# Rows folded by symmetry behind the row transforms, column transforms as fp32 pairs in array halves

## The chip, the core and the metric
The kernel runs on one core of one Trainium2 chip. TensorE (PE in the profile) multiplies matrices, its weight loads are listed as PEld; VectorE is DVE, ScalarE is ACT, GpSimd is POOL, and SyncE (SP) issues DMAs, the copies between DRAM and on-chip memory (SBUF; TensorE writes into PSUM). All times are device microseconds (us). The metric is the time of one execution of the whole program. fp32r is a single-pass form of fp32 on TensorE with less precision; fp32 proper takes two instructions of two passes each per product.

## The reference
Input x is (8, 56, 56, 256), fp32: eight images of 56 rows of 56 positions, 256 channels. One block of three residual layers is computed; the change is in the first.

```python
x = x + conv(_gn(x), ...)            # group normalisation, then the layer below
t = tokens(x)
t = t + attention(_ln_t(t), ...)     # not touched
t = t + ffn(_ln_t(t), ...)           # not touched

def conv(x, ...):
    xn = simple_rms(x)
    u = silu(xn @ W_u.T + b_u)       # 512 channels, a gate
    v = silu(xn @ W_v.T + b_v)       # 512 channels
    g = rpe_coeffs(...)              # small MLP over the 111 x 111 offsets: 512 numbers each
    a = zeros(112, 112); a[offsets mod 112] = g
    vf = rfft2(v, s=(112, 112)); af = rfft2(a)
    y = irfft2(vf * af)[:56, :56]    # per channel: a long convolution over the image
    return (u * y) @ W_o.T + b_o + x
```

The Fourier transforms are matrix products with cosines and sines. Only 56 of the 112 row frequencies are carried, each as a real and an imaginary plane, so a transformed image has 112 rows (ROWS) for 56 (SIDE).

## The kernel before
The program is six phases, one after another, with a barrier of all engines between them; each phase writes its results to DRAM for the next. Within a phase every engine has its own instruction list, written out by hand in the order in which it runs, and semaphores tie the lists together. The change touches the first four phases.

**Kernel rows** (`kernel_rows_phase`, names kr_). The MLP runs over all offsets in 14 steps of eight rows, `u` = 0 and 1 of four (RPE_ROWS) each. GpSimd casts the coordinates of four rows (`take_points`, L306), TensorE's `first_layer` (L383) takes them, deeper layers follow, with scales that VectorE computes in a chain of small operations (L547 to L559). The tail of a step has eight rows: TensorE makes the coefficients, VectorE adds the bias (L649) and makes the low part (L633, both inputs in SBUF), TensorE transforms along the row (`row_pass`), ScalarE copies out (`take_row`, L487), and SP stores four rows at a time (L296, kern_rows). Group normalisation's statistics are taken beside it.

**Project** (`project_phase`, pr_). 56 chunks of eight image rows, four tiles `t` of two rows each. GpSimd normalises (L1047, L1051), TensorE transposes (L1064) and multiplies with W_v, VectorE scales and adds the bias (L1220, here "bias"), ScalarE applies silu (L1142, "gate"), TensorE transforms along the row: one product for each of the tile's two rows, on array row halves (L1084, contraction over 56 partitions, from 0 and from 64). ScalarE copies out one row (L1148), VectorE the other (L1228), and SP stores the chunk (L1004, v_rows). VectorE also makes low parts of the transposed x (L1212, twice a chunk).

**Columns** (`columns_phase`, co_). For each of 56 row frequencies k: the taps of the convolution's kernel are transformed along the column (four products of 111 x 512 into `taps_ps`), ScalarE copies them to `spec`. For each image b of eight: forward column transform, product with the spectrum (complex: VectorE multiplies L902 and L904, GpSimd subtracts and adds L925 and L928), inverse transform (L806, L808), copy (ScalarE L862), store. The forward and taps products go as high and low fp32r parts, three passes each by the helper `product` (L135): ScalarE makes the high part (L837, L841), VectorE the low (L882, L887). SP loads v (L736) and taps (L732), and stores y (L742) for each pair of images.

**Mix** (`mix_phase`, mx_). 56 chunks again: x is loaded and normalised anew on GpSimd (L1429, L1433), the gate u is made, TensorE transforms back along the row (L1485, array column halves), VectorE multiplies with the gate (L1710), TensorE transposes (L1495) and multiplies with W_o, and residual and layer norm follow (residual: GpSimd L1442, L1445).

## Time and profile before

| | |
|---|---|
| median of 3 runs | 5410.76 us (5406.27 to 5413.85) |
| profiled execution | span of its instructions 5398.1 us, its only time |
| kernel rows | first 690 us |
| project | to about 1285 us |
| columns | to about 2860 us |
| mix | to about 3930 us |
| busy over the span | PE 97%, DVE 74%, ACT 47%, POOL 46% |

The profile is of one execution. In a line of the page's groups, `L902 DVE TENSOR_TENSOR co_direct<-co_v_ps,co_spec ... x448` is line 902 of the program, the engine, the operation, what it writes and reads, and how often it ran; then the busy time, the mean of one in ns, and the time the engine was idle before it. In a timeline the first number is the start, the second how long the group of instructions ran; an engine can overlap the end of one operation with the start of the next, so that starts of VectorE's operations stand closer than their durations. An idle time with an arrow names who ended it.

### The profile page before, as it was taken

Reading aid. Unit: us, or ns where it says so; the run is one execution under the profiler, and the core shown is the slowest. Engines: PE = TensorE matmul, PEld = TensorE weight load, DVE = VectorE, ACT = ScalarE, POOL = GpSimd, SP = SyncE. Lnnn points to the kernel's source line nnn. Section 1 sums busy time; section 2 is a strip of 40 time slices with the busy share of each in tenths; the row PEclk is TensorE's granted clock in tenths of the full one; section 3 lists DMA queues with packets and bytes.
Section 4 is the critical chain, followed back from the end, with each engine's and each line's share of the span. In section 5 each row is a group of like instructions: output and inputs, shape, how many; then the busy total and the mean of one; then the engine's idle time right before and its main releaser. Section 6 shows DMA issues by size and latency. Waiting matters only on the chain. (4 is left out here: it accounts for less than half of the span.)

```text
span 5398.1 us, 89326 instructions
## 1 busy us (share of the span) xinstructions
PE 5214.1 (97%) x27048; PEld 3662.3 (68%) x27048; DVE 3997.7 (74%) x6176; ACT 2512.3 (47%) x4791; POOL 2489.9 (46%) x1381
## 2 busy tenths in 40 slices
PE   8999899997999999999998999999989999987999
PEld 6777655554555555555556777777767777765999
DVE  6777666666999999999996676766635666665887
ACT  5555577774434334343434555555532222211555
POOL 0000054443999999999995555555301111111332
PEclk9999999998999999999999999999999999998999
DMA  3222167775444444444446666666533333433443
GB/s 109 89 89 72 53 197 219 217 217 170 149 150 150 149 152 148 152 148 150 151 136 182 195 203 200 191 200 202 163 113 97 104 113 107 118 89 97 123 122 113
DMA packets 349121, 782.62 MB, mean 145 GB/s; under 512 B 43433, under 2 KB 147845, under 8 KB 339460
## 3 DMA queue, kind: packets, MB, share of 16 engines
q1 hardware_dynamic: 326596, 703.91, 44.2%
q10 hardware_dynamic: 22400, 77.08, 4.0%
q8 instruction: 73, 1.20, 0.1%
q14 instruction: 52, 0.43, 0.0%
HBM read 420.49 MB, written 360.38 MB: 145 GB/s over the span
## 5 line engine op out<-in xcount | busy, mean ns | idle before, releaser
L928 POOL TENSOR_TENSOR co_prod<-co_cross 111x512 f32<-111x512 f32 x448 | 848.8, 1895 | 0.0
L862 ACT ACTIVATE co_y_out<-co_y_ps 112x512 f32<-112x512 f32 x448 | 267.9, 598 | 928.2 <-PE co_y_ps L808 923.1
L925 POOL TENSOR_TENSOR co_prod<-co_direct 111x512 f32<-111x512 f32 x448 | 576.3, 1286 | 203.8 <-PE co_y_ps L808 116.0
L902 DVE TENSOR_TENSOR co_direct<-co_v_ps,co_spec 111x1024 f32<-111x1024 f32 x448 | 543.5, 1213 | 92.0 <-PE co_v_ps L135 87.9
L2012 POOL TENSOR_TENSOR at_t<-at_t,at_p_bias 112x1024 f32<-112x1024 f32 x56 | 137.7, 2470 | 889.3 <-DMA at_t<-t_tiles 889.3
L904 DVE TENSOR_TENSOR co_cross<-co_v_ps,co_spec 111x1024 f32<-111x1024 f32 x448 | 541.5, 1209 | 0.0
L135 PE MATMUL co_v_ps<-co_v_high,co_col_fwd_high 112*111 112x512 f32 x896 | 506.1, 565 | 1.4 <-DVE co_cross L904 1.4
L806 PE MATMUL co_y_ps<-co_prod,co_col_inv 111*112 111x512 f32 x896 | 458.2, 592 | 0.0
L808 PE MATMUL co_y_ps<-co_prod,co_col_inv 111*112 111x512 f32 x896 | 457.5, 592 | 0.1
L882 DVE TENSOR_TENSOR co_v_low<-co_v_in,co_v_high 112x1024 fp32r<-112x1024 f32 x224 | 372.3, 1662 | 0.0
L135 PE MATMUL co_v_ps<-co_v_low,co_col_fwd_high 112*111 112x512 f32 x896 | 354.3, 395 | 0.0
L2173 ACT ACTIVATE at_qk_t<-at_bank_ps 128x448 f32<-128x448 f32 x224 | 121.6, 543 | 499.1 <-PE at_bank_ps L135 499.1
L135 PE MATMUL co_v_ps<-co_v_high,co_col_fwd_low 112*111 112x512 f32 x896 | 349.1, 390 | 0.0
L1596 ACT ACTIVATE mx_mixed_high<-mx_turn_ps 128x448 fp32r<-128x448 f32 x224 | 121.8, 544 | 431.1 <-PE mx_turn_ps L1495 431.1
L808 PEld LDWEIGHTS co_y_ps<-co_prod,co_col_inv 111*112 111x112 f32 x896 | 156.0, 175 | 229.3 <-issue 212.3
L1220 DVE SCALAR_TENSOR_TENSOR pr_v_pre<-pr_v_ps,pr_inv,pr_v_bias 120x512 f32<-120x512 f32 x224 | 167.6, 748 | 150.8 <-PE pr_v_ps L135 145.5
L1442 POOL TENSOR_TENSOR mx_resid<-mx_x_in,mx_o_bias 112x1024 f32<-112x1024 f32 x56 | 134.0, 2393 | 311.2 <-DVE mx_t L1726 311.2
L306 POOL CAST kr_points<-kr_coords 6x448 fp32r<-6x448 f32 x28 | 15.2, 568 | 565.8 <-DMA kr_coords<-coords 565.8
L2502 POOL TENSOR_TENSOR ff_base<-ff_t,ff_n 112x1024 f32<-112x1024 f32 x56 | 132.7, 2370 | 301.3 <-DVE ff_out L2663 281.5
L1047 POOL TENSOR_TENSOR pr_gx<-pr_x_in,gn_rows 128x1024 f32<-128x1024 f32 x55 | 133.0, 2419 | 298.1 <-DMA pr_x_in<-x 298.1
L135 PE MATMUL mx_o_ps<-mx_w_o_high,mx_mixed_high 128*112 128x256 f32 x896 | 252.3, 282 | 3.5 <-DVE mx_mixed_low L1715 3.5
L135 PE MATMUL mx_o_ps<-mx_w_o_high,mx_mixed_low 128*112 128x256 f32 x896 | 252.2, 281 | 0.0
(277 smaller groups left out, 14268.5 us busy)
## 6 DMA issues: line engine op xcount, KB each, us to landing
v_rows<-pr_rows_out SPq DMA_DIRECT2D x56, 1792.0 KB, 8.2
co_v_in<-v_rows SPq DMA_DIRECT2D x448, 224.0 KB
y_rows<-co_y_out SPq DMA_DIRECT2D x448, 224.0 KB
mx_y_in<-y_rows SPq DMA_DIRECT2D x224, 448.0 KB, 5.5
kr_x_in<-x SPq DMA_DIRECT2D x56, 448.0 KB, 3.9
kern_rows<-kr_rows_out SPq DMA_DIRECT2D x28, 896.0 KB, 4.7
pr_x_in<-x SPq DMA_DIRECT2D x112, 224.0 KB
mx_x_in<-x SPq DMA_DIRECT2D x56, 448.0 KB, 5.3
```

What stands on the lines that cost most here:

```text
L135: last = nc.tensor.matmul(out, weights[a], data[b], start=start and i == 0, stop=stop and i == len(passes) - 1)
L806: nc.tensor.matmul(y_ps[b % 2][:2 * SIDE, :], col_inv[:, 0, :], prod[b % 2][:, :WIDE], start=True, stop=False)
L808: nc.tensor.matmul(y_ps[b % 2][:2 * SIDE, :], col_inv[:, 1, :], prod[b % 2][:, WIDE:], start=False, stop=True).then_inc(inv_mm, 1)
L862: nc.scalar.activation(y_out[:, b, :], y_ps[b % 2][:2 * SIDE, :], ACT.Copy).then_inc(y_ready, 1)
L882: nc.vector.tensor_tensor(v[1][:, images, :], v_in[:, images, :], v[0][:, images, :].bitcast(F32), ALU.subtract).then_inc(low_v, 1)
L902: nc.vector.tensor_tensor(direct[b % 2][:], v_ps[b % 2][:POINTS, :], spec[i][:, :2 * WIDE], ALU.mult).then_inc(real_terms, 1)
L904: nc.vector.tensor_tensor(cross[b % 2][:], v_ps[b % 2][:POINTS, :], spec[i][:, WIDE:], ALU.mult).then_inc(multiplied, 1)
L925: nc.gpsimd.tensor_tensor(prod[b % 2][:, :WIDE], direct[b % 2][:, :WIDE], direct[b % 2][:, WIDE:], ALU.subtract).then_inc(real_ready, 1)
L928: nc.gpsimd.tensor_tensor(prod[b % 2][:, WIDE:], cross[b % 2][:, :WIDE], cross[b % 2][:, WIDE:], ALU.add).then_inc(combined, 1)
L1220: nc.vector.scalar_tensor_tensor(out=v_pre[t % 2][:], in0=v_ps[t % 2][:SPAN, :], scalar=inv[:SPAN, j % GROUP * TILES + t:j % GROUP * TILES ...
L1442: nc.gpsimd.tensor_tensor(resid[u][:], x_in[u][:], o_bias[:].unsqueeze(1).to_broadcast(each), ALU.add).then_inc(resid_part, 1)
L2012: nc.gpsimd.tensor_tensor(t1[j % HELD][:], t1[j % HELD][:], p_bias[:].unsqueeze(1).to_broadcast([TILE, TILES, CH]), ALU.add).then_inc(t1_b ...
```

## The change
The image rows are reordered on the host, so that each chunk of eight rows holds mirrored pairs (row i and row 55 - i), and back on the way out. A row transform's result of a pair is then folded: the sum goes to one slot, the difference to another. The fold of the sum has a real plane, that of the difference is written with real and imaginary planes exchanged, so that a store of a chunk is three DMAs. The offsets of the kernel are ordered in mirrored pairs as well.

With folded rows the forward column transform needs one product over 56 rows for each of the two halves of the input, not a complex one over 112, and likewise the inverse.

- Kernel rows: GpSimd folds (`fold_rows`, two operations of 112 x 1024 for four rows) from `rows_out` into `taps_out`; SP stores `taps_out` in three pieces; ScalarE's `take_row` waits for the fold.
- Project: the row product writes 1024 columns per tile; ScalarE copies an even tile (`take_first`), VectorE adds and subtracts the odd one (`fold_rows`, two operations of 112 x 1024). The normalised x (gx) is stored too.
- Columns: no high and low parts. The forward transform is two fp32 products over 56 partitions each (0 to 55 and 64 to 119, array row halves), the inverse two products of 56 output columns (array column halves), the taps two full fp32 products. VectorE multiplies once per image, 2048 columns, with the PSUM operand repeated; GpSimd adds once, 1024 columns. For image 5 GpSimd does nothing and TensorE sums the terms in PSUM with four products. Rings of four, lag of three images. ScalarE copies four parts of the spectrum.
- Mix: gx is loaded, not computed. The odd result is copied by ScalarE (`take_odd`), VectorE adds and subtracts (`unfold`, 4 operations of 120 x 512 a chunk), GpSimd multiplies with the gate (`mix`, four of 120 x 512). TensorE has the same products in another order.

```diff
# kernel rows, GpSimd
+                def fold_rows(s, u):
+                    n = s * 2 + u
+                    pool.wait_ge(row_out, RPE_ROWS * (n + 1))
+                    pool.wait_ge(stored[u], 16 * PIECES * s)
+                    pair = rows_out[u][:].rearrange("p (m r) n -> p m r n", r=2)
+                    for parity, op in enumerate((ALU.add, ALU.subtract)):
+                        nc.gpsimd.tensor_tensor(taps_out[u][:, parity * MIRRORS:(parity + 1) * MIRRORS, :], pair[:, :, 0, :],
+                                                pair[:, :, 1, :], op).then_inc(folded, 1)
+
                 for s in range(STEPS):
                     for u in range(2):
                         take_points(s, u)
+                        if s:
+                            fold_rows(s - 1, u)
+                for u in range(2):
+                    fold_rows(STEPS - 1, u)
# project, VectorE and ScalarE
-                def take_row(s, j, t):
-                    nc.vector.tensor_copy(rows_out[j % 2][:, 2 * t + 1, :], row_ps[t % 2][1][:ROWS, :]).then_inc(row1_out, 1)
+                def fold_rows(s, j, pair):
+                    dve.wait_ge(first_out, 1 + n + 1)
+                    dve.wait_ge(row_mm, 2 * n + 2)
+                    nc.vector.tensor_tensor(out[:, slots(0, pair), :].rearrange("p r n -> p (r n)"), first[pair][:],
+                                            row_ps[1][:ROWS, :], ALU.add)
+                    nc.vector.tensor_tensor(out[:, slots(1, pair), :].rearrange("p r n -> p (r n)"), first[pair][:],
+                                            row_ps[1][:ROWS, :], ALU.subtract).then_inc(folded, 1)
+                def take_first(s, j, pair):
+                    act.wait_ge(row_mm, 2 * n + 1)
+                    act.wait_ge(folded, n)
+                    nc.scalar.activation(first[pair][:], row_ps[0][:ROWS, :], ACT.Copy).then_inc(first_out, 1)
# columns, SP
+                def stored(k, pair):
+                    sp.wait_ge(y_ready, SLOTS + k * BATCH + 2 * pair + 2)
+                    store_y(sp, k, pair)
                 def step(k, i, more, more2):
                     for pair in range(PAIRS):
+                        if more and pair + 1 < PAIRS:
+                            next_v(k, 1, pair + 1)
+                        if more2 and pair + 1 == PAIRS:
+                            sp.wait_ge(taps_mm, k + 2)
                             load_taps(sp, k, 2)
+                            next_v(k, 2, 0)
+                        stored(k, pair)
# columns, TensorE
+                    for part in range(2):
+                        side = slice(part * GAP, part * GAP + SIDE)
+                        last = nc.tensor.matmul(v_ps[b % 2][:POINTS, bass.ts(part, WIDE)], col_fwd[side, :], v_in[side, b, :],
+                                                start=True, stop=True)
+                        for part in range(2):
+                            last = nc.tensor.matmul(y_ps[b % 2][part * GAP:part * GAP + SIDE, :],
+                                                    col_inv[:, part * SIDE:(part + 1) * SIDE],
+                                                    prod[b % RING][:, bass.ts(part, WIDE)], start=True, stop=True)
                     for b in range(LAG, BATCH):
-                        if b == BATCH // 2 + 1 and more:
-                            spectrum(k + 1)
+                        if more and b <= LAG + 1:
+                            spectrum(k + 1, b - LAG)
                         forward(k, b)
                         inverse(k, b - LAG)
# columns, VectorE and GpSimd
+                        twice = [POINTS, 2, 2 * WIDE]
+                        nc.vector.tensor_tensor(terms[b % RING][:].rearrange("p (t n) -> p t n", t=2),
+                                                v_ps[b % 2][:POINTS, :].unsqueeze(1).to_broadcast(twice),
+                                                spec[i][:].rearrange("p (t n) -> p t n", t=2), ALU.mult).then_inc(multiplied, 1)
+                    for b in POOLED:
+                        pair = terms[b % RING][:].rearrange("p (t s n) -> p t s n", t=2, s=2)
+                        nc.gpsimd.tensor_tensor(prod[b % RING][:].rearrange("p (t n) -> p t n", t=2), pair[:, :, 0, :], pair[:, :, 1, :],
+                                                ALU.add).then_inc(combined, 1)
```

GpSimd's list in kernel rows, before: nothing but casts of coordinates, one for each `u`.

```order
L306 CAST kr_points0<-kr_coords0 6x448
L306 CAST kr_points1<-kr_coords1 6x448
L306 CAST kr_points0<-kr_coords0 6x448
L306 CAST kr_points1<-kr_coords1 6x448
L306 CAST kr_points0<-kr_coords0 6x448
```

And of the changed kernel, from its first step on:

```order
L336 CAST kr_points0<-kr_coords0 6x448
L336 CAST kr_points1<-kr_coords1 6x448
L336 CAST kr_points0<-kr_coords0 6x448
L344 ISA
L344 TENSOR_TENSOR kr_taps_out0<-kr_rows_out0 112x1024 x2
L336 CAST kr_points1<-kr_coords1 6x448
L344 TENSOR_TENSOR kr_taps_out1<-kr_rows_out1 112x1024 x2
L336 CAST kr_points0<-kr_coords0 6x448
```

From the second step on, a fold of the step before stands between the cast of points 0 and that of points 1.

VectorE's list in project, before (L1220 is the bias, L1212 the low parts, L1228 the copy of row results; register instructions are waits whose value is computed):

```order
L1220 SCALAR_TENSOR_TENSOR pr_v_pre<-pr_v_ps,pr_inv,pr_v_bias 120x512
L1209 REGISTER_ALU
L1212 TENSOR_TENSOR pr_x_t_low<-pr_xt_ps,pr_x_t_high 128x480 x2
L1218 REGISTER_ALU
L1220 SCALAR_TENSOR_TENSOR pr_v_pre<-pr_v_ps,pr_inv,pr_v_bias 120x512
L1227 REGISTER_ALU
L1228 COPY pr_rows_out<-pr_row_ps 112x512 x2
L1218 ISA
L1220 SCALAR_TENSOR_TENSOR pr_v_pre<-pr_v_ps,pr_inv,pr_v_bias 120x512
L1218 REGISTER_ALU
L1220 SCALAR_TENSOR_TENSOR pr_v_pre<-pr_v_ps,pr_inv,pr_v_bias 120x512
L1228 COPY pr_rows_out<-pr_row_ps 112x512 x2
```

And of the changed kernel (L1259 is the bias, L1251 the low parts, L1270 and L1272 the fold):

```order
L1259 SCALAR_TENSOR_TENSOR pr_v_pre<-pr_v_ps,pr_inv,pr_v_bias 120x512
L1257 REGISTER_ALU
L1259 SCALAR_TENSOR_TENSOR pr_v_pre<-pr_v_ps,pr_inv,pr_v_bias 120x512
L1265 REGISTER_ALU
L1266 ISA
L1270 TENSOR_TENSOR pr_rows_out<-pr_first,pr_row_ps 112x1024
L1272 TENSOR_TENSOR pr_rows_out<-pr_first,pr_row_ps 112x1024
L1257 REGISTER_ALU
L1259 SCALAR_TENSOR_TENSOR pr_v_pre<-pr_v_ps,pr_inv,pr_v_bias 120x512
L1248 REGISTER_ALU
L1251 TENSOR_TENSOR pr_x_t_low<-pr_xt_ps,pr_x_t_high 128x480 x2
L1257 REGISTER_ALU
```

The fold stands where the two copies stood, twice as wide, and reads what ScalarE's `take_first` wrote.

SP's list in columns, before, around a taps load (L732; L736 loads v, L742 stores y):

```order
L732 DMA co_taps_in<-kern_rows 111x512
L732 ISA
L732 DMA co_taps_in<-kern_rows 111x512
L716 REGISTER_ALU
L742 ISA
L742 DMA y_rows<-co_y_out 56x2x512
```

And of the changed kernel (L770 taps, L774 v, L780 y):

```order
L780 DMA y_rows<-co_y_out 56x2x512
L780 ISA
L780 DMA y_rows<-co_y_out 56x2x512
L805 REGISTER_ALU
L770 ISA
L770 DMA co_taps_in<-kern_rows 112x512
L770 ISA
L770 DMA co_taps_in<-kern_rows 112x512
L793 ISA
L774 ISA
L774 DMA co_v_in<-v_rows 56x2x512
```

Before, the load is ahead of the store of images 2 and 3 and asks for low parts made early in the frequency; now it stands behind the store of images 4 and 5 and ahead of the next frequency's first v load.

## Rows read from the trace of the kernel before

**Rows 1.** Windows: length; busy PE, PEld, DVE, ACT, POOL; PE clock, DMA share, GB/s
```profile
0.00:690.00 690.00, 649.26 (x4618) 492.03 (x4620) 486.90 (x997) 368.94 (x713) 31.81 (x42) 0.99 0.28 83
690.00:1285.00 595.00, 580.86 (x2648) 343.82 (x2648) 382.41 (x609) 458.23 (x1060) 251.77 (x105) 0.99 0.69 213
1285.00:2860.00 1575.00, 1546.67 (x5156) 900.14 (x5156) 1459.04 (x1185) 617.19 (x900) 1405.17 (x901) 0.99 0.48 148
2860.00:3930.00 1070.00, 1043.65 (x6716) 797.95 (x6716) 726.70 (x1515) 593.19 (x1008) 530.74 (x223) 0.99 0.66 194
```

**Rows 2.** The taps tile: instructions, ns min/median/max, first and last start
```profile
L732 SPq MOVE co_taps_in<-kern_rows x108: 29/29/29, 1319.3 to 2779.2; - x108
```

**Rows 3.** Timeline of columns, 2000 to 2030: start, length, instructions
```profile
2002.40 1.02 PE L806 MATMUL co_y_ps<-co_prod,co_col_inv 111*112 111x512 f32 x2
...
2004.32 0.60 ACT L862 ACTIVATE co_y_out<-co_y_ps 112x512 f32<-112x512 f32 x1 [2.50 <-PE co_y_ps L808]
...
2005.09 0.88 SPq L742 DMA_DIRECT2D y_rows<-co_y_out  x2
...
2005.49 1.02 PE L806 MATMUL co_y_ps<-co_prod,co_col_inv 111*112 111x512 f32 x2
```

**Rows 4.** The v_rows tensor: its stores in project, first and last start
```profile
L1004 SPq DMA_DIRECT2D v_rows<-pr_rows_out x56: 316/356/364, 697.8 to 1271.8; - x56
```

**Rows 5.** Timelines of project, from 1001, and of mix, from 3504
```profile
1004.42 1.21 DVE L1212 TENSOR_TENSOR pr_x_t_low<-pr_xt_ps,pr_x_t_high 128x480 fp32r<-128x480 f32 x2
...
1005.03 1.97 PE L1084 MATMUL pr_row_ps<-pr_v,pr_row_fwd 56*112 56x512 f32 x8
...
1006.94 0.50 PE L135 MATMUL pr_v_ps<-pr_w_v_high,pr_x_t_high 128*120 128x512 f32 x1
...
3506.71 1.93 PE L1485 MATMUL mx_y_ps<-mx_y_in,mx_row_inv 112*56 112x512 f32 x8
```

**Rows 6.** Groups by line and shape: count, busy us, mean ns, idle before
```profile
L902 DVE TENSOR_TENSOR co_direct<-co_v_ps,co_spec 111x1024 f32<-111x1024 f32 x448 | 543.5, 1213 | 92.0 <-PE co_v_ps L135 87.9 <-ACT co_spec L846 4.1
...
L928 POOL TENSOR_TENSOR co_prod<-co_cross 111x512 f32<-111x512 f32 x448 | 848.8, 1895 | 0.0
...
L1442 POOL TENSOR_TENSOR mx_resid<-mx_x_in,mx_o_bias 112x1024 f32<-112x1024 f32 x56 | 134.0, 2393 | 311.2 <-DVE mx_t L1726 311.2
```

**Rows 7.** Timeline of columns, 2016 to 2021, VectorE and GpSimd
```profile
2016.50 1.30 POOL L925 TENSOR_TENSOR co_prod<-co_direct 111x512 f32<-111x512 f32 x1 [0.57 <-PE co_y_ps L808]
...
2016.94 1.93 DVE L882 TENSOR_TENSOR co_v_low<-co_v_in,co_v_high 112x1024 fp32r<-112x1024 f32 x1
...
2017.76 2.27 POOL L928 TENSOR_TENSOR co_prod<-co_cross 111x512 f32<-111x512 f32 x1
```

**Rows 8.** The page's DMA issues: count, KB each, median us from issue to landing
```profile
n_tok<-mx_n ACTq DMA_DIRECT2D x56, 448.0 KB, 3.1
...
mx_y_in<-y_rows SPq DMA_DIRECT2D x224, 448.0 KB, 5.5
```

**Rows 9.** Groups by line and shape: bias, gate and a wide ScalarE read of PSUM
```profile
L1220 DVE SCALAR_TENSOR_TENSOR pr_v_pre<-pr_v_ps,pr_inv,pr_v_bias 120x512 f32<-120x512 f32 x224 | 167.6, 748 | 150.8 <-PE pr_v_ps L135 145.5 <-DVE pr_inv L1205 5.2
...
L1142 ACT ACTIVATE pr_v<-pr_v_pre 120x512 f32<-120x512 f32 x222 | 140.0, 631 | 120.8 <-DVE pr_v_pre L1220 120.1
...
L470 ACT ACTIVATE kr_square<-kr_t_ps 128x896 f32<-128x896 f32 x112 | 102.8, 918 | 146.7 <-PE kr_t_ps L398 130.0 <-PE kr_t_ps L383 16.6
```

**Rows 10.** Timeline of kernel rows, 288 to 303: end of a step, start of the next
```profile
290.95 0.34 SPq L296 DMA_DIRECT2D kern_rows<-kr_rows_out  x1
...
291.23 0.68 DVE L633 TENSOR_TENSOR kr_coef_low<-kr_coef,kr_coef_high 111x512 fp32r<-111x512 f32 x1
...
294.04 0.49 PE L135 MATMUL kr_row_ps<-kr_coef_high,kr_row_taps_high 111*112 111x512 f32 x1 [0.22 <-DVE kr_coef_low L633]
...
294.93 0.67 PE L383 MATMUL kr_t_ps<-kr_points,kr_w_in_both 6*128 6x448 f32 x2
...
302.15 0.27 DVE L547 SCALAR_TENSOR_TENSOR kr_scale<-kr_scale,kr_root 128x112 f32<-128x112 f32 x1
```

518 lines of the change are left out of this document (254 added, 264 removed).

## The prediction

> **What bounds the kernel now.** I read the stage windows first [rows 1]: in the four stages that the change touches TensorE is busy 649 of 690, 581 of 595, 1547 of 1575 and 1044 of 1070 us, and no other engine comes near it, except in the column stage, where VectorE has 1459 and GpSimd 1405 us. The granted clock is 0.99 in all four, the 2.4 GHz level. So TensorE sets the end everywhere; its work is where time can be won, and the question for the other engines is whether they stay below it. Second, the period of each loop. Columns: a row frequency every 27.55 us (the moves in front of the taps loads, two per frequency, run from 1319.3 to 2779.2 over 54 frequencies: 1459.9/53 [rows 2]); an image every 3.09 us, 2005.49 − 2002.40 [rows 3]. Project: 56 stores from 697.8 to 1271.8, 574.0/55 = 10.44 us a chunk [rows 4]. Kernel rows: 14 steps in the first 690 us, mix: 56 chunks in 1070 us [rows 1].
>
> **Columns: TensorE's work.** An image now costs six single-pass products of 0.23 us and two fp32 products of 0.86 us. After the change both transforms are fp32 pairs in the two halves of the array. How long is such a pair? In the project stage two tiles make eight instructions on row halves from 1005.03 to 1006.94 [rows 5]: 1.91 us for four products of 512 columns; one after another they would take 4 × 0.86 = 3.4, two at a time 1.71, so the halves do run together, and 0.2 is left for the way in and out. Column halves do the same: eight in 1.93 us [rows 5]. I take 0.854 for a pair and 0.17 for each change of array shape. No row shows a change from row halves straight to column halves; the bounds are 0.1 and 0.3.
> Per image: 2 × 0.854 + 2 × 0.17 = 2.05, eight of them 16.4. Image 5 has one more pair, 0.85. The taps' spectrum is two full products, 1.71, and two more changes, 0.34. Sum **19.3 us** a frequency (with 0.1 and 0.3 for a change: 18.0 and 21.6).
>
> **Columns: the others.** VectorE had two products of 1.21 per image [rows 6] and a split of two images' input in every second one. It gets one product of 2048 columns; back-to-back ones of 1024 start 1.13 apart, so 2.20 to 2.28, times eight 17.6 to 18.2: below 19.3, by little. That it reads PSUM twice over is shown by no row; the bounds are 2.2 and, at half speed, 4.4 (rival c), and 2.2 is taken because width alone set the time of the others. GpSimd had 1.30 and 1.90 per image for operations of the same width [rows 6, 7]; the second is long where VectorE's split, with both inputs in SBUF, lies beside it: the split of 2016.94 lasts 1.93 and goes on past the end of GpSimd's at 2017.80, and GpSimd's next, from 2017.76, lasts 2.27 instead of 1.30 [rows 7]. The splits go. One GpSimd operation of 1024 columns takes 2.39 [rows 6]; seven, with 0.1 for each handover, 17.4: below 19.3 too. ScalarE: eight copies of 0.60 and four of the spectrum. Three engines stand within 10% of each other and the ring of four with a lag of three lets them drift, so TensorE stays the bound.
> One wait is new. The taps load of frequency k+2 is issued behind the store of images 4 and 5, and TensorE wants it after image 7's inverse. From the end of inverse 5: ScalarE's copy 0.04 + 0.60, store issue 0.17 later (2004.92 to 2005.09 [rows 3]), 0.88 for its two issues [rows 3], then the load, 448 KB: transfers of that size landed after 3.1 and 5.5 us (medians [rows 8]); I take 3.6, near the lower, as the DMA share here is 0.48 against 0.66 in mix [rows 1]. Together 5.3, with 0.05 more to TensorE 5.4, while TensorE has forward, inverse, forward, inverse, 4 × 1.025 = 4.1. Stall **1.3 us** a frequency (0.8 with 3.1, 3.2 with 5.5). Before, the load had a whole frequency of room.
> So 20.6 a frequency: (27.55 − 20.6) × 56 = −389, and −8 for the splits and the wait for them at the stage's start. Range −479 (19.0 a frequency) to −339 (21.5).
>
> **Project.** TensorE's work stays. The loop that closes is between VectorE and ScalarE. Before, eight copies of 512 columns, four on each, emptied the row product, and each depended only on its own tile. Now ScalarE copies a pair's even tile (1024 columns: 0.918 for 896 [rows 9], so 1.01) and VectorE folds with 2 × 1.13 = 2.26. In the order of the instructions: bias 3 (0.75 [rows 9]) → gate 3 (0.63 [rows 9]) → first 0 (1.01) → fold 0 (2.26) → bias 0 and 1 (1.50) → gate 1 (0.63) → first 1 (1.01) → fold 1 (2.26) → bias 2 (0.75) → low parts (1.21 [rows 5]) → bias 3. Each waits for the one before it, on its engine or by a semaphore: 12.01, and six handovers of 0.04, 12.25 a chunk; with the reciprocal of every second chunk 12.35. Against 10.44 of now that is +1.9, × 56 = **+106**. It would be +40 if part of it hides (the low parts, 1.21, beside a wait of ScalarE), +120 if ScalarE's table loads join it. The stores of three pieces and gx (448 KB a chunk more) go by a queue that waits; the DMA share is 0.69 now [rows 1].
>
> **Kernel rows.** GpSimd gets two operations of 1024 columns per four rows, 4.8 us, twice a step; its own share is small. But its order is cast, fold, cast, fold, so the cast of the next step's second coordinates stands behind the fold. The fold starts when row 4 of the step is out, 290.95, and ends 295.9; with the cast behind it (0.6) TensorE's first layer, which stands at 294.93 [rows 10], starts 1.7 us late. And VectorE's operations with two SBUF inputs did not run beside GpSimd's in the column stage; each waited the other out [rows 7]. At 291.23 the low part of a coefficient, two SBUF inputs, becomes ready beside the fold [rows 10]; it waits to 293.5, GpSimd's second waits 0.7 for it, the next low part waits again to 296.6, and the row product of 294.04 [rows 10] follows at 297.3: 3.3 late, which contains the 1.7. The second fold, from 301.7, meets the scale of a layer (302.15, two SBUF inputs [rows 10]) and costs up to 2.4 more. 5.7 a step × 14 = +80; the last fold and store +5. I take **+82**; bounds +20 (the queue's 1.7 alone, × 14 = 24, some of it hidden) and +100. (The Trainium skill has a rule against this part: SBUF — State Buffer, SBUF: two separate sides, says that the port pair of VectorE and GpSimd is an exclusive lock, held for the whole instruction by whichever of them starts first. The rows at 2016.94 and 2017.76 agree. Where two engines only shared a rate, the wait of the 14 steps would be near the queue's +24 + 5 = +29; by the rule it is the +82 above.)
>
> **Mix.** TensorE's work is the same; GpSimd loses two normalising operations of 2.39 and gets four products of half the width; ScalarE gets 2 × 0.6 beside a half-idle engine (593 of 1070 [rows 1]); the gx load adds 448 KB to a stage at 0.66 of DMA [rows 1]. The gated tile now comes by one more engine (a copy, an unfold, GpSimd's product) but TensorE's order asks for it later. I take +0.2 a chunk, **+12**; bounds −5 and +45.
>
> **Sum.** −389 − 8 + 106 + 82 + 12 = −197. The profiled execution has a span of 5398.1 us; the median of three runs is 5410.76, 12.7 more, for what lies around the span. The change is the same on either: 5398.1 − 197 + 12.7 = **5214 us**.
>
> **Rivals.** (a) *TensorE alone sets it*: no stall for the taps and no lock in kernel rows. Columns 19.3 (−462 − 8), project +60, kernel rows +24 + 5, mix 0: 5030 us. For it: the rings, and that folds are off TensorE. Against it: the order of the queues, and [rows 7]. Chance 0.15.
> (b) *GpSimd sets the columns*: its wide operation takes what its two took together, 1.30 + 1.90 = 3.20 [rows 6, 7]. 7 × 3.2 = 22.4 a frequency, −288 − 8; with the rest, 5315. For it: this is how it runs there now. Against it: VectorE's two-SBUF operations are gone. Chance 0.12.
> (c) *Slower than before*: VectorE's product reads PSUM twice over by a stride of zero. Ran it at half speed, 4.4 an image, a frequency would take 35.2: (35.2 − 27.55) × 56 = +428, and with −8 and the +200 of the other stages 6031 us. The point from which it decides is nearer: the other stages' +200 − 8 = 192 are 3.4 a frequency, so the change loses where a frequency takes more than 24.1, a product of VectorE more than 3.0. Against it: a product's time went by its width in every form seen, 1.21 with PSUM [rows 6]. Chance 0.08.
> (d) *The change doesn't win where it says*: the loops of project and kernel rows take more than the sum (each its upper bound, 120 + 100 + 45 = 265) and the columns 21.5, −339 − 8: 5329. Chance 0.07. My forecast has 0.58.
>
> **Range and chances.** From 5080 (columns at 19.3 with part of the losses outside: −470 + 140 = −330) to 5340 (columns at 21.5 with the losses outside, or rival b and a little). Rival (a)'s core and (c) stay out. Faster by over 0.2% (11 us, about what a measurement tells from no change): all but (c) and 0.01: 0.91; within 0.2%: 0.01; slower 0.08.
>
> **What would show it.** Of the changed kernel: taps loads 20.6 us apart, and TensorE idle about 1.3 before the taps' product with a DMA as releaser; VectorE's product at 2.2 to 2.3, GpSimd's at 2.4; stores of v 12.3 apart; in kernel rows VectorE's low part of a coefficient stretched to 2 us or more, the steps 5.7 longer. Wrong would be: GpSimd's sum over 2.7 (rival b), VectorE's product over 2.5 (rival c), pairs that end 1.7 apart, project at 10.5 (the loop isn't closed), or steps of kernel rows longer by under 2 (the engines' meeting costs nothing).

## The result, and the profile after

The changed kernel takes 5494.41 us (median of four runs, 5492.59 to 5500.43); the kernel before, timed beside it, 5409.88. The ratio is 1.0163, 95% interval 1.0151 to 1.0175: slower by 1.6%. The prediction was 5214, with 5080 to 5340 as its range: wrong in sign and outside the range. The profiled execution has a span of 5494.0 us against 5398.1, so 95.9 us are to be explained. (The prediction added 12.7 us for what lies around the span; here the profiled execution took 5495.8 us, 1.8 more than its span. So about 11 of the 12.7 were the difference between one execution and the median.)

The table sets the stages side by side, each cut at an event that both kernels have (the first move in front of a taps load stands half a frequency later in the changed kernel; cut at the very first taps load, 1280.5 and 1484.3, project would be +117 and columns −218). The middle columns are from the trace, the last is the sum of the prediction.

| stage, cut at | before | after | difference | predicted |
|---|---|---|---|---|
| kernel rows, to the last store of kern_rows | 661.1 | 748.0 | +87 | +82 |
| project, to the first move of the taps loads | 658.2 | 773.2 | +115 | +106 |
| columns, to the first load of y in mix | 1536.8 | 1320.4 | −216 | −397 |
| mix, to the last load of y | 1004.7 | 1106.8 | +102 | +12 |
| what follows (not changed) | 1537.3 | 1545.6 | +8 | 0 |
| sum | 5398.1 | 5494.0 | +96 | −197 |

Two of the four terms came near what was worked out, one of them with some luck, as said below. Two did not, and together they are 271 of the 293 us by which the forecast of the span missed. Windows of the changed kernel by stage (length; busy PE, PEld, DVE, ACT, POOL; clock, DMA share, GB/s), which answer to [rows 1]:

```profile
0.00:760.00 760.00, 669.14 (x4576) 494.26 (x4576) 571.61 (x987) 358.72 (x681) 163.80 (x92) 0.96 0.25 73
760.00:1482.00 722.00, 618.58 (x2688) 347.84 (x2688) 493.57 (x619) 467.22 (x980) 264.30 (x110) 0.98 0.70 214
1482.00:2845.00 1363.00, 1179.46 (x4036) 266.19 (x4036) 1001.84 (x453) 377.45 (x673) 915.90 (x396) 0.92 0.58 172
2845.00:3990.00 1145.00, 1060.01 (x6664) 779.33 (x6664) 719.94 (x1489) 631.70 (x1102) 547.34 (x336) 1.00 0.71 198
```

Before, TensorE was busy in 94 to 98% of each of these stages. Now it is idle for 91, 103, 184 and 85 us of them, no other engine has more than 76% in any, and the granted clock of the columns is 0.92 instead of 0.99. A stage in which no engine is full is set by a chain that passes through several of them.

**Columns.** TensorE's own work is as worked out. The two starts of L855, the inverse transform, are 2.05 us apart, as the sum of four array halves and their changes said; VectorE's product and GpSimd's sum have their expected lengths (groups by line and shape: count, busy us, mean ns, idle before):

```profile
2107.84 1.07 PE L855 MATMUL co_y_ps<-co_prod,co_col_inv 111*56 111x512 f32 x4
...
2109.89 1.07 PE L855 MATMUL co_y_ps<-co_prod,co_col_inv 111*56 111x512 f32 x4
```

```profile
L926 DVE TENSOR_TENSOR co_terms<-co_v_ps,co_spec 111x2048 f32<-111x2048 f32 x448 | 999.8, 2284 | 340.7 <-PE co_v_ps L837 328.0
L944 POOL TENSOR_TENSOR co_prod<-co_terms 111x1024 f32<-111x1024 f32 x392 | 915.3, 2358 | 480.3 <-DVE co_terms L926 478.9
```

With 2284 and 2358 ns both engines wait over 300 us for the one ahead of them: neither rival (b) nor (c) happened. What did is in the tile of the loaded taps (its moves, the register instructions in front of the loads; who waited for it: us, times), and in the timeline around one wait:

```profile
L770 SPq MOVE co_taps_in<-kern_rows x108: 29/29/29, 1521.2 to 2788.4; - x108
...
  PE co_taps_ps L826: 156.5, 55
```

```profile
2101.02 1.97 PE L826 MATMUL co_taps_ps<-co_taps_in,co_col_taps 112*111 112x512 f32 x2 [3.96 <-DMA co_taps_in<-kern_rows]
...
2102.92 1.91 PE L837 MATMUL co_v_ps<-co_v_in,co_col_fwd 56*111 56x512 f32 x4
...
2105.76 1.11 PE L826 MATMUL co_taps_ps<-co_taps_in,co_col_taps 112*111 112x512 f32 x2
...
2106.80 1.11 PE L837 MATMUL co_v_ps<-co_v_in,co_col_fwd 56*111 56x512 f32 x4
```

A frequency takes (2788.4 − 1521.2)/53 = 23.91 us. TensorE waits for the taps 55 times, 2.85 us each. And the first two groups behind the wait take 1.97 and 1.91 where the same instructions take 1.11 later. The windows of this place say why: no matmul from 2098 to 2101, then a granted clock of 0.54, near the lower of its two levels (1.2 GHz), then 1.00 (2.4 GHz) again.

```profile
2098.00:2101.00 3.00, 0.00 (x0) 0.00 (x0) 0.65 (x1) 0.00 (x0) 3.00 (x2) 1.00 0.82 249
2101.00:2104.70 3.70, 3.68 (x6) 0.82 (x6) 0.00 (x0) 0.00 (x0) 0.53 (x1) 0.54 0.21 82
2104.70:2120.00 15.30, 15.30 (x62) 3.53 (x60) 14.21 (x7) 5.53 (x10) 9.83 (x5) 1.00 0.54 156
```

**Mix.** The timeline of one chunk shows which engines hand to each other (start, length, instruction, idle before and releaser). Its first half, around VectorE's shift:

```profile
3492.20 1.28 ACT L1633 ACT_TABLE_LOAD   x1 [1.51 <-DVE mx_u_pre L1754]
...
3494.03 0.58 ACT L1639 ACTIVATE mx_odd<-mx_y_ps 120x512 f32<-120x512 f32 x1
...
3494.64 1.29 DVE L1762 TENSOR_TENSOR mx_gated<-mx_y_ps,mx_odd 120x512 f32<-120x512 f32 x2 [1.88 <-ACT mx_odd L1639]
...
3495.41 2.52 POOL L1490 TENSOR_TENSOR mx_gated<-mx_gated,mx_gate 120x512 f32<-120x512 f32 x2 [6.60 <-DVE mx_gated L1762]
...
3497.17 0.78 DVE L1802 SCALAR_TENSOR_TENSOR mx_shift<-mx_moments,mx_inv 112x4 f32<-112x4 f32 x1
...
3498.12 1.09 ACT L1654 ACTIVATE mx_n<-mx_t,mx_shift,mx_inv 112x256 f32<-112x256 f32 x2 [2.64 <-DVE mx_shift L1802]
```

Its second half, to where TensorE waits:

```profile
3499.64 0.52 ACT L1645 ACTIVATE mx_mixed_high<-mx_turn_ps 128x448 fp32r<-128x448 f32 x1
3500.19 0.62 DVE L1767 TENSOR_TENSOR mx_mixed_low<-mx_turn_ps,mx_mixed_high 128x448 fp32r<-128x448 f32 x1 [1.58 <-ACT mx_mixed_high L1645]
...
3501.40 0.60 PE L1507 MATMUL mx_turn_ps<-mx_ident,mx_gx 112*128 112x112 f32 x4 [1.23 <-DVE mx_n_t L1808]
```

The unfold (VectorE, L1762) waits for ScalarE's copy of the odd half; that copy stands behind a gate and its table load; the shift (L1802), which is four columns wide, takes 0.78 beside GpSimd's product where it took 0.16 before; ScalarE's normalising waits 2.64 for it; the next gate (3499.12), the next mixed tile, VectorE's low part and its copy of the turned n (3500.74) follow; and there TensorE waits. A chunk takes 20.5 us; the copy of the same odd half comes at 3484.59 and again at 3505.14. By the lengths of the stages, 1004.7 to 1106.8, it took 18.6 before. The list of waits from 2900 to 3900 (who waited for what: us, times, longest) confirms it in sum:

```profile
ACT mx_gate L1633 <- DVE mx_u_pre L1754: 149.7, 50, 3.1
ACT mx_n L1654 <- DVE mx_shift L1802: 131.4, 49, 2.8
DVE mx_gated L1762 <- ACT mx_odd L1639: 91.5, 49, 2.0
```

**Kernel rows.** The lock on which the +82 rested is there (timeline around a fold of kernel rows; the low part of a coefficient took 0.68 before [rows 10]):

```profile
325.68 5.17 POOL L344 TENSOR_TENSOR kr_taps_out<-kr_rows_out 112x1024 f32<-112x1024 f32 x2 [26.95 <-ACT kr_rows_out L530]
325.91 2.70 DVE L676 TENSOR_TENSOR kr_coef_low<-kr_coef,kr_coef_high 111x512 fp32r<-111x512 f32 x1
...
328.67 0.48 PE L157 MATMUL kr_row_ps<-kr_coef_high,kr_row_taps_high 111*112 111x512 f32 x1 [1.39 <-DVE kr_coef_low L676]
329.19 2.20 DVE L676 TENSOR_TENSOR kr_coef_low<-kr_coef,kr_coef_high 111x512 fp32r<-111x512 f32 x1
```

The two low parts, each with two SBUF inputs, stretch over the end of one GpSimd instruction each, and TensorE waits behind the first and, in a row not shown, behind the second. (The Trainium skill, SBUF — State Buffer, Who interferes with whom, says that VectorE's second SBUF input comes through the read interface that GpSimd reads by; the rows agree, with 2.70 and 2.20 us for an operation of 0.68.)

The lower clock is in this stage too. Of the 540 us from 100 to 640 TensorE is idle 49.5 in the changed kernel and 6.6 in the one before, and the granted clock is 0.97 against 1.00 (the kernel before first):

```profile
100.00:640.00 540.00, 533.43 (x3857) 404.79 (x3856) 397.36 (x830) 296.44 (x568) 11.89 (x22) 1.00 0.25 76
```

```profile
100.00:640.00 540.00, 490.54 (x3350) 359.81 (x3349) 426.86 (x729) 261.81 (x500) 120.68 (x63) 0.97 0.25 70
```

**Project.** The stores of v are 12.44 us apart (12.35 predicted), and the timeline shows the hand-overs of the closed loop:

```profile
1106.05 1.01 ACT L1185 ACTIVATE pr_first<-pr_row_ps 112x1024 f32<-112x1024 f32 x1
...
1107.29 1.22 DVE L1270 TENSOR_TENSOR pr_rows_out<-pr_first,pr_row_ps 112x1024 f32<-112x1024 f32 x1 [1.81 <-ACT pr_first L1185]
...
1109.56 1.40 DVE L1259 SCALAR_TENSOR_TENSOR pr_v_pre<-pr_v_ps,pr_inv,pr_v_bias 120x512 f32<-120x512 f32 x2
1109.79 1.12 PE L1121 MATMUL pr_row_ps<-pr_v,pr_row_fwd 56*112 56x512 f32 x4 [0.75 <-DVE pr_rows_out L1272]
1110.41 1.29 ACT L1179 ACTIVATE pr_v<-pr_v_pre 120x512 f32<-120x512 f32 x2 [1.83 <-DVE pr_v_pre L1259]
```

### The profile page after: what moved, and what is told of

It is laid out like the page before. It is cut to its first block and busy times, and to the rows that moved or that the text cites. A ratio compares the mean times of both kernels' runs of the same rounds, so it can differ in the third digit from the quotient of the medians.

```text
span 5494.0 us, 86154 instructions
## 1 busy us (share of the span) xinstructions
PE 4932.3 (90%) x25928; PEld 3025.3 (55%) x25928; DVE 3741.9 (68%) x5446; ACT 2321.8 (42%) x4565; POOL 2161.3 (39%) x1047
## 5 line engine op out<-in xcount | busy, mean ns | idle before, releaser
L926 DVE TENSOR_TENSOR co_terms<-co_v_ps,co_spec 111x2048 f32<-111x2048 f32 x448 | 999.8, 2284 | 340.7 <-PE co_v_ps L837 328.0
L944 POOL TENSOR_TENSOR co_prod<-co_terms 111x1024 f32<-111x1024 f32 x392 | 915.3, 2358 | 480.3 <-DVE co_terms L926 478.9
L901 ACT ACTIVATE co_y_out<-co_y_ps 120x512 f32<-120x512 f32 x448 | 267.5, 597 | 959.0 <-PE co_y_ps L855 857.6
L837 PE MATMUL co_v_ps<-co_v_in,co_col_fwd 56*111 56x512 f32 x1792 | 541.0, 683 | 1.8 <-DVE co_terms L926 1.8
L1490 POOL TENSOR_TENSOR mx_gated<-mx_gated,mx_gate 120x512 f32<-120x512 f32 x224 | 283.3, 1286 | 587.0 <-DVE mx_gated L1762 587.0
L855 PE MATMUL co_y_ps<-co_prod,co_col_inv 111*56 111x512 f32 x1568 | 452.3, 657 | 2.0 <-POOL co_prod L944 2.0
L1121 PE MATMUL pr_row_ps<-pr_v,pr_row_fwd 56*112 56x512 f32 x896 | 243.5, 628 | 49.8 <-DVE pr_rows_out L1272 48.0
L1270 DVE TENSOR_TENSOR pr_rows_out<-pr_first,pr_row_ps 112x1024 f32<-112x1024 f32 x112 | 136.8, 1221 | 200.6 <-ACT pr_first L1185 198.3
L855 PEld LDWEIGHTS co_y_ps<-co_prod,co_col_inv 111*56 111x56 f32 x1568 | 76.5, 136 | 339.6 <-issue 295.1
L157 PE MATMUL mx_o_ps<-mx_w_o_low,mx_mixed_high 128*112 128x256 f32 x896 | 251.9, 281 | 0.0
L2640 ACT ACTIVATE ff_hid<-ff_hid_ps,ff_fc_bias 128x224 f32<-128x224 f32 x448 | 185.4, 447 | 123.1 <-PE ff_hid_ps L2562 120.0
L2116 PE MATMUL at_bank_ps<-at_keys,at_n_tok 112*128 112x256 f32 x896 | 232.2, 383 | 5.6 <-DVE at_keys L2368 5.6
```

The lines of the kernel that those rows point to most:

```text
L157: last = nc.tensor.matmul(out, weights[a], data[b], start=start and i == 0, stop=stop and i == len(passes) - 1)
L837: last = nc.tensor.matmul(v_ps[b % 2][:POINTS, bass.ts(part, WIDE)], col_fwd[side, :], v_in[side, b, :], start=True, stop=True)
L855: last = nc.tensor.matmul(y_ps[b % 2][part * GAP:part * GAP + SIDE, :], col_inv[:, part * SIDE:(part + 1) * SIDE], prod[b % RING][:, bass. ...
L901: nc.scalar.activation(y_out[:, b, :], y_ps[b % 2][:SPAN, :], ACT.Copy).then_inc(y_ready, 1)
L926: nc.vector.tensor_tensor(terms[b % RING][:].rearrange("p (t n) -> p t n", t=2), v_ps[b % 2][:POINTS, :].unsqueeze(1).to_broadcast(twice), ...
L944: nc.gpsimd.tensor_tensor(prod[b % RING][:].rearrange("p (t n) -> p t n", t=2), pair[:, :, 0, :], pair[:, :, 1, :], ALU.add).then_inc(comb ...
```

## The experiments

The theory after reading the two traces: four causes in four stages that don't touch each other, each an order of instructions on one engine and not an amount of work. For the columns, where the taps load is issued; for project, where ScalarE copies the first half; for mix, where VectorE makes the shift; for kernel rows, the reads of GpSimd's fold and the casts queued behind it. The rivals: transfers that are slow wherever they are issued, GpSimd or TensorE as the bound, and in kernel rows only one of the two. The single experiments change the changed kernel in one place; where one stands on top of others, it says so. "k" below is the time of one row frequency in the columns.

### The taps load at pair 1 instead of after the last pair

```diff
-                        if more2 and pair + 1 == PAIRS:
+                        if more2 and pair == 1:
                             sp.wait_ge(taps_mm, k + 2)
                             load_taps(sp, k, 2)
+                        if more2 and pair + 1 == PAIRS:
                             next_v(k, 2, 0)
```

> The changed kernel with one edit: SyncE issues the taps load of frequency k+2 ahead of the store of images 2 and 3, as the kernel before did, and no longer behind the store of images 4 and 5. Theory A, the load's place in the queue costs twice: TensorE waits 2.85 us a frequency for it, and 1.8 more go to a lower granted clock behind that idle time. Then a frequency falls from 23.9 to 19.3 to 19.5 us, the granted clock of the column stage rises from 0.92 to 0.97 or more, and the whole is 240 to 260 us faster than the changed kernel's 5494: about 5245. Theory B, the DMA engines are full (share 0.58, transfers land later): the wait only moves to a load of v or a store, and a frequency stays above 22.

Measured: 5243.39 us, ratio to the kernel before 0.9696 (0.9668 to 0.9725); k is 19.34 against 23.91. The window of the columns, and who waited for the taps tile:

```profile
1500.00:2300.00 800.00, 800.00 (x2982) 185.10 (x2980) 739.52 (x332) 278.91 (x499) 677.99 (x290) 1.00 0.70 213
```

```profile
  PE co_taps_ps L827: 0.4, 1
```

TensorE is busy all the time, the clock is at 1.00, nobody waits for the taps, and 251 us are gone: one moved issue turns a kernel that is 1.6% slower than the one before into one that is 3.0% faster. The DMA share rises to 0.70, so the transfers were not the limit. 19.34 is also the first direct measurement of the sum "16.4 + 0.85 + 1.71 + 0.34 = 19.3": the step was right to 0.04. Of the 4.57 us that are gone per frequency, 2.85 are the wait and 1.7 the slow groups behind it (1.97 and 1.91 instead of twice 1.11 is 1.66).

### The shift's inputs earlier on VectorE, in mix

```diff
                         measure(*before, 0)
+                    if before2:
+                        invert(*before2)
                     if now:
...
                         residual(*before, 1)
-                    if before2:
-                        invert(*before2)
                     if after:
```

> The changed kernel with one edit: in mix VectorE makes the layer norm's inverse and shift before the second unfold, not behind it and the residual. Theory A, VectorE and ScalarE are in a closed chain of waits in mix, in which the shift stands late and waits for GpSimd's product besides (0.78 us where it needs 0.16): the chunk falls from 20.6 to about 19.2 us, the shift's mean to 0.2, the whole by about 80 us to 5415. Theory B, the loads (y lands 8.2 us after its issue, 5.5 before) set the chunk: it stays at 20.6.

Measured: 5427.13 us, ratio 1.0045 (1.0027 to 1.0063); mix 1044.3 instead of 1106.8, 19.3 us a chunk. `invert` (the reciprocal and the shift) now stands ahead of the unfold that frees GpSimd's next product, so GpSimd isn't in it any more. The edit does two things at once, it moves the shift forward in VectorE's list and takes it out from beside GpSimd's product; the second is worth 0.59 us a chunk by the two rows below, and of the 1.2 us gained how much each gave was not separated. The group of the shift, here and in the changed kernel:

```profile
L1802 DVE SCALAR_TENSOR_TENSOR mx_shift<-mx_moments,mx_inv 112x4 f32<-112x4 f32 x56 | 9.1, 162 | 1.9
```

```profile
L1802 DVE SCALAR_TENSOR_TENSOR mx_shift<-mx_moments,mx_inv 112x4 f32<-112x4 f32 x56 | 42.0, 750 | 1.9
```

The loads of y in mix land after 7.5 us here, 8.2 in the changed kernel and 5.5 before [rows 8]; the stage got 62 us shorter with them nearly as late, so they are not what it waited for. 40 us of the loss remained, and one thing more of the same chain was taken up in the kernel with all repairs below.

### Project: ScalarE's second copy ahead of the gates

```diff
                             square(s, j + 3, t)
+                    take_first(s, j, 1)
                     for t in range(LAG):
...
                     for t in range(LAG, TILES):
-                        if t % 2 == 0:
-                            take_first(s, j, t // 2)
                         if left >= 3:
```

> The changed kernel with one edit: in project ScalarE copies the second pair's even tile before the two gates of the next chunk, not behind them. Theory A, the chain bias 3, gate 3, first 0, fold 0, bias 0 and 1, gate 1, first 1, fold 1, bias 2 is closed and sets the chunk: the edit cuts it between the first gate's bias and the second fold, the chunk falls from 12.44 to 10.4 to 10.6 us, TensorE's time, the whole by about 105 us to 5390. Theory B, the wide operations on VectorE or the longer stores and gx (DMA share 0.70) set it: the chunk stays above 12.

Measured: 5429.28 us, ratio 1.0037 (1.0026 to 1.0049); the stores are 11.15 us apart, and had been expected at 10.4 to 10.6. Moving this one copy gave back two thirds of the loss and not all of it. The waits of GpSimd for SP's queue, which stores gx, were the next suspect.

### The same, with the store of gx two chunks ahead

```diff
+                for j in range(2):
+                    sp.wait_ge(gx_ready, j + 1)
+                    store_gx(0, j)
...
-                    store_gx(s, j)
+                    if left >= 2:
+                        sp.wait_ge(gx_ready, s * GROUP + j + 3)
+                        store_gx(s + (j + 2) // GROUP, (j + 2) % GROUP)
```

> The kernel with ScalarE's copy ahead of the gates (11.15 us a chunk), and one edit more: SyncE stores gx two chunks earlier, ahead of the row stores it waited behind. Theory A, what was left over TensorE's 10.4 was this: GpSimd overwrites gx only when its store has landed (316 us of waiting in 50 chunks), ScalarE's squares wait for GpSimd (98 us) and hold the copies behind them: the chunk falls to 10.45 to 10.7. Theory B, the DMA engines are at their limit (share 0.80): the chunk stays at 11.0 or more.

Measured: 5416.28 us, ratio 1.0013 (1.0003 to 1.0023); the stores are 11.11 apart, against 11.15, where the expectation had 10.45 to 10.7. That theory fell. In a stretch of 300 us the GpSimd wait for the store of gx had been the largest in the list (169.0 us, 27 times), and it was only replaced by one for x of the same length (170.3, 27 times). The 13 us between the two medians are not in the chunks, which account for 2: the columns took 18.6 us less in the profiled execution, where TensorE's waits for the taps were 2.75 us each instead of 2.97; why they were shorter is open.

What remains is in the timeline of the kernel with the first repair. In every second chunk ScalarE loads two tables, the second of them ahead of gates 2 and 3, and the first copy stands behind both gates:

```profile
1118.78 1.28 ACT L1179 ACT_TABLE_LOAD   x1
...
1120.08 1.27 ACT L1179 ACTIVATE pr_v<-pr_v_pre 120x512 f32<-120x512 f32 x2
1121.25 1.01 ACT L1185 ACTIVATE pr_first<-pr_row_ps 112x1024 f32<-112x1024 f32 x1
```

### Kernel rows: four kernels for two suspects

The casts ahead of both folds, so that no cast is queued behind one:

```diff
                     for u in range(2):
                         take_points(s, u)
-                        if s:
+                    if s:
+                        for u in range(2):
                             fold_rows(s - 1, u)
```

> The changed kernel with one edit: in kernel rows GpSimd casts both coordinates of a step before it folds the step before. Theory A, the fold holds up VectorE's operations with two inputs in SBUF, wherever it stands: a step stays about 52 us, the last store stays at 748 +- 5 us. Theory B, the cast behind the fold costs 1.7 us a step: the last store comes at about 724. Theory C, all of it is the queue: it comes at about 666.

Measured: 5505.58 us, ratio 1.0181 (1.0148 to 1.0215); the last store of kern_rows at 744.3 against 748.0. No gain to speak of.

The folds replaced by constant fills of the same length, which read nothing (the taps that the later stages load are then a constant, so the fold is left out of what is computed):

```diff
-                    for parity, op in enumerate((ALU.add, ALU.subtract)):
-                        nc.gpsimd.tensor_tensor(taps_out[u][:, parity * MIRRORS:(parity + 1) * MIRRORS, :], pair[:, :, 0, :],
-                                                pair[:, :, 1, :], op).then_inc(folded, 1)
+                    for i in range(5):
...
+                        last = nc.gpsimd.memset(taps_out[u][:, parity * MIRRORS:(parity + 1) * MIRRORS, :], 0.001).then_inc(spent, 1)
...
```

> The changed kernel with the fold of kernel rows left out: in its place GpSimd fills the same buffer with a constant, five times 512 x 2 columns, about as long (5.0 us) and at the same place in its queue, but reading nothing from SBUF; the spectrum of the taps is then a constant's. Theory A, GpSimd's reads of SBUF shut out VectorE's operations with two SBUF inputs: without them VectorE's low part of a coefficient (mean of two inputs, 0.68 before the change) goes back to 0.68 to 0.75, and the last store comes near 700, later than 661 only by what the queue costs (1.7 a step) or less. Theory B, the cast's place behind the fold or the longer store does it: the last store stays at 740 to 750.

Measured: 5471.98 us (one run); last store at 724.1, between what the two theories had (near 700; 740 to 750). VectorE's low part is back at its old length, beside a GpSimd that works as long as with the folds, but its casts to the high part are not (340 ns; 542 in the changed kernel, 225 in the kernel before):

```profile
L681 DVE TENSOR_TENSOR kr_coef_low<-kr_coef,kr_coef_high 111x512 fp32r<-111x512 f32 x112 | 76.4, 682 | 0.6
...
L600 DVE CAST kr_scale_high<-kr_scale 128x112 fp32r<-128x112 f32 x84 | 28.6, 340 | 2.9
```

```profile
PE kr_t_ps L431 <- POOL kr_points L337: 21.7, 11, 2.1
```

TensorE waits for the points instead (the second fence: its waits from 100 to 640), 1.97 us each time, which is near the 1.7 a step that the prediction gave the queue. But the stage is 63 us longer than in the kernel before, and 14 such waits are 28. The windows show the rest, the whole stretch and the one behind a wait that ended at 316.68:

```profile
100.00:640.00 540.00, 511.95 (x3471) 385.48 (x3471) 375.57 (x756) 269.27 (x515) 118.78 (x131) 0.94 0.26 73
```

```profile
316.60:320.00 3.40, 3.32 (x8) 2.31 (x8) 1.90 (x4) 1.79 (x3) 0.03 (x1) 0.50 0.86 260
```

TensorE is idle 28.0 us of the 540, 6.6 before, and the granted clock is 0.94 against 1.00: as in the columns, a wait is followed by products at the lower of the two levels. So neither suspect alone is cheap. Each of them, left alone, holds most of the time or all of it: 83 us with the casts first, 63 with nothing read. So both at once, the two diffs above together:

> The changed kernel with the fold of kernel rows left out, five constant fills in its place as before (last store 724), and both casts ahead of them. Theory A, the fold costs by two ways that lie beside each other, its reads that shut out VectorE and its place ahead of the cast; taking one away (744 with the casts first, 724 with nothing read) leaves the other, and only both together give the time back: the last store comes at 664 to 675. Theory B, a third cost is left, GpSimd's fills or the longer store: it stays above 700.

Measured: 5412.7 us (one run); last store at 665.7, the whole loss but 5 us, as expected. Taking away one cost gives 4 or 24 us, taking away both 82. VectorE's casts take 340 ns here too (mean of the same group), so their lengthening by the fills cost nothing to speak of.

And the fold on VectorE, in four parts between its operations of the next step, where GpSimd has only its casts (the function fold_rows moves to VectorE with it; the call alone is shown):

```diff
                         next_scale(s, n)
+                        if 3 <= n < 7 and has_before(s):
+                            fold_rows(s - 1, n - 3)
```

> The changed kernel with the fold of kernel rows on VectorE, one of the four operations of a step behind each of the layers 3 to 6 of the next step, GpSimd casting alone. Theory A, the meeting of the two engines costs 80 us: VectorE has room (572 of 760 us), 4.9 us a step more on it cost 0.7 us on the path; the last store comes at about 675 to 685, the whole is about 65 us faster than the changed kernel, 5430. Theory B, VectorE's own chain is as tight: the last store stays above 720.

Measured: 5407.07 us, ratio 0.9999 (0.9989 to 1.001); last store at 668.5, where 675 to 685 had been expected. The group says what GpSimd's 2.4 us are on VectorE:

```profile
L673 DVE TENSOR_TENSOR kr_taps_out<-kr_rows_out 112x1024 f32<-112x1024 f32 x56 | 67.9, 1217 | 0.0
```

This is the real repair, as the fold is computed: −87 us, 79.5 of them by the last store, and the stage is back within 8 us of the kernel before.

### All repairs together

The five edits above (taps, shift, second copy, gx, folds on VectorE), and in mix one more on VectorE, `scale_gate` of tile 3 ahead of the two low parts, so that ScalarE's gate with its table load starts earlier:

```diff
                         low_part_mixed(*before, 3)
+                    if now:
+                        scale_gate(*now, 3)
                     if after:
                         low_part_x(*after, 1)
                     if now:
                         low_part_mixed(*now, 0)
-                        scale_gate(*now, 3)
```

> The changed kernel with all of it: the taps load early, the fold of kernel rows on VectorE, ScalarE's copy and the gx store early in project, and in mix the inverse and shift before the second unfold and also the fourth tile's bias ahead of the low parts. If the causes add up: last kernel row store 680, project 10.5 a chunk, columns 19.35 a frequency, mix 18.5 to 18.7 a chunk (19.2 with the inverse alone), that is 5494 - 245 - 68 - 108 - 110 = 4963 us, against 5410 of the kernel before. If the stages meet a common limit, the DMA engines, project and mix stay above 11 and 19: 5020 or more.

Measured: 4984.27 us, ratio 0.9224 (0.9208 to 0.9239). The single repairs were worth 251.0, 67.3, 65.1 and 87.3 us (the store of gx, whose 13 us were not in the chunks, is left out), 470.7 in all, which leaves 5023.7; the rest, 39 us, is mix, now 1002.7 instead of 1044.3, below the 1004.7 of the kernel before. The stages add up. The expectation, 4963, was missed by 21: it had 10.5 us for a chunk of project, which takes 11.13 (some 35 us in all), and 680 for the last store of kernel rows, which came at 666.7.

### ScalarE's first copy between gates 2 and 3

```diff
+                    gate(s, j, 2, n * TILES)
+                    take_first(s, j, 0)
+                    gate(s, j, 3, n * TILES)
```

(in place of both gates ahead of it; the four squares follow, then the second copy and the next chunk's gates 0 and 1)

> The kernel with everything moved (4984 us, project 11.13 a chunk), and one edit more in project: ScalarE copies the first pair's even tile between the gates 2 and 3, and makes all squares before the second copy. Theory A: what is left over TensorE's 10.4 is a chain that goes through gate 3, behind which the first copy stands, and through the table load in front of gate 2, which in every second chunk starts only when that gate's input is there (1.28 us). Out of the chain the chunk falls to 10.2 to 10.5, the whole to about 4945. Theory B, the DMA engines (share 0.80) or the two single row pairs (1.12 each instead of 1.97 for two) set it: it stays at 11.0 or more.

Measured: 4964.23 us, ratio 0.9189 (0.9172 to 0.9207); stores 10.69 apart, against 11.13. The expectation, 10.2 to 10.5, was missed by 0.2 and the direction was right. In a stretch of 300 us TensorE is now counted busy in 298.74 (289.92 before this edit):

```profile
900.00:1200.00 300.00, 298.74 (x1349) 174.34 (x1348) 243.78 (x308) 227.74 (x491) 134.46 (x56) 1.00 0.83 257
```

Why a chunk takes 10.69 all the same, and not 10.44 [rows 4]? In this stretch every second chunk takes 10.50 to 10.52 us, as every chunk does in the kernel before (10.51 there between two starts of TensorE's transposes), and the others 10.79 to 11.03. The whole difference lies in TensorE's row products: a group of two tiles takes 1.97 in the short chunks and up to 2.32 in the long ones.

```profile
929.88 1.21 DVE L1275 TENSOR_TENSOR pr_rows_out<-pr_first,pr_row_ps 112x1024 f32<-112x1024 f32 x1
930.04 2.32 PE L1129 MATMUL pr_row_ps<-pr_v,pr_row_fwd 56*112 56x512 f32 x8
```

VectorE's fold ends at 931.09, and the weights of the group's second tile, whose product goes to the buffer that this fold reads, are loaded at 931.21 (a row not shown). So TensorE still waits a little for the fold in every second chunk, within a group that counts as busy. The DMA share is 0.83 here, and whether the 448 KB more a chunk cost anything was not tried.

### No image summed on TensorE

```diff
-        SUMMED_BY_PE = (5,)
+        SUMMED_BY_PE = ()
```

> The kernel with everything moved (4984 us, columns 19.34 a frequency), with GpSimd adding the terms of all eight images and TensorE of none. TensorE saves one pair, 0.85 us a frequency, GpSimd gets an eighth operation: 8 x (2.36 + 0.13) = 19.9. Theory A, without the one image that TensorE sums GpSimd becomes the bound of the columns: 19.7 to 20.1 a frequency, the whole 20 to 40 us slower. Theory B, GpSimd still hides: 18.5 a frequency, the whole 47 us faster.

Measured (on top of all repairs, without the last edit): 4963.21 us, ratio 0.9182 (0.9164 to 0.9201); k is 18.68 against 19.34. The expectation's theory A, GpSimd at 19.7 to 20.1, fell: it had put 0.13 us of handover to each of GpSimd's operations. Theory B had 18.5 and 47 us; the whole is 21 us faster, less than the 37 of 56 frequencies at 0.66 (the columns' part of the span fell by 31). Without the extra pair TensorE's sum is 19.3 − 0.85 = 18.5; GpSimd's eight operations start 16.30/7 = 2.33 us apart, 18.6. The windows show GpSimd full:

```profile
2048.74 16.30 POOL L946 TENSOR_TENSOR co_prod<-co_terms 111x1024 f32<-111x1024 f32 x7
```

```profile
1500.00:2300.00 800.00, 796.62 (x2916) 182.38 (x2914) 761.37 (x344) 288.54 (x515) 798.46 (x344) 1.00 0.73 221
```

TensorE's sum of one image relieves an engine that, once the taps come in time, doesn't need it: it costs 0.66 us a frequency. Both engines are within 0.2 us of the period, TensorE busy in 796.62 of 800 us and GpSimd in 798.46; by these sums the bound is GpSimd's, by 0.1.

### Everything

All repairs, with both of the last two diffs.

> All repairs together, with ScalarE's order of the run before the last one in the project stage (gate 2, first copy 0, gate 3, squares, first copy 1), and in the columns no image summed on TensorE: GpSimd adds all eight. The two last edits lie in stages that do not overlap in time. Theory A, stages add up: columns 18.68 us a frequency as in the kernel that had this edit alone on top of the others (19.34 without it), project 10.69 a chunk, 4964 - 21 = 4943 us, ratio to the kernel before 0.914. Theory B, the stage that follows pays back what the columns gain, since the DMA traffic of the columns is squeezed: 4955 to 4965, no gain over either.

Measured: 4934.73 us (4930.58 to 4944.26), ratio 0.9128 (0.9112 to 0.9144): 8.7% faster than the kernel before and 10.2% faster than the changed one. k is 18.68, a chunk of project 10.69; the two edits add up to 49.5 us under the kernel with all repairs, of which 20.0 and 21.1 had been measured apart. The 8 us in excess are within the spread of these runs.

## Why the prediction was wrong, point by point

- **"Columns: TensorE's work", 19.3 a frequency: right.** 19.34 was measured once the wait for the taps was out of the way. So was what it said of VectorE (2.28) and GpSimd (2.36 for 2.39), and rivals (b) and (c) fell by these rows.
- **"One wait is new", 1.3 us a frequency: the mechanism was right, its size was wrong, and this is the largest error: 181 of 293 us.** It has two parts. First the wait itself, above all the landing (timeline of the changed kernel, another frequency). The sum took 3.6 us for the load, "near the lower" of 3.1 and 5.5. Here SP issues it at 2119.90 and TensorE's product starts at 2124.94:

```profile
2119.90 1.16 SPq L770 DMA_DIRECT2D co_taps_in<-kern_rows  x2
...
2124.94 1.99 PE L826 MATMUL co_taps_ps<-co_taps_in,co_col_taps 112*111 112x512 f32 x2 [2.88 <-DMA co_taps_in<-kern_rows]
```

  5.0 us. The DMA share had been the argument for 3.6, but it is a mean over the whole stage of the kernel before; just where the load is issued a store and a load of v stand beside it, and the share from 2098 to 2101, with this load in it, is 0.82. That the neighbours made it slow is likely and not shown; no run moved them alone. The upper row, 5.5, would have been the nearer one. (The Trainium skill, SBUF — State Buffer, The DMA setup-cost knee, fits a transfer by about 2 us and its bytes by 436 GB/s; for 448 KB that would be an estimate of some 3.1 us, where the rows show 5.0 beside other transfers, and none shows this load alone.) The other 0.2 us are SP's: the load is issued 1.13 us behind the store of images 4 and 5, where the sum had 0.88. The wait became 2.85 instead of 1.3: 1.55 × 56 = 87 us. Second, what the prediction had no term for: a wait of this length brings the clock down to 0.54 for the next 3.7 us, another 1.7 us a frequency, 94 us. The prediction's own upper bound for the stall, 3.2, held the 2.85; but its range for the columns ended at 21.5 a frequency, which leaves only 2.2 for a stall on top of 19.3. So the wait alone, 19.3 + 2.85 = 22.2, was already beyond that range, and the slow groups carried it on to 23.9.
- **Kernel rows, +82: right in sum (+87), right in its mechanism, with luck in its prices.** That the cast's queue is contained in the lock's cost is shown: casts first gives back 4. But the steps were to be 5.7 us longer by waits; TensorE's idle time rose by 42.9 us in the 540 from 100 to 640, some ten steps, so about 4.2 a step, and the rest is the lower clock (0.97), for which the sum had no term. For the queue alone it had 24 + 5, and the kernel with nothing read shows 63, through the same missing term. And its own parts, 80 and 5, are 85, of which it took 82. Rival (a), without the lock, fell by the same runs.
- **Project, +106: right (+115; 12.44 against 12.35 a chunk).** The loop of the two engines was read from the order of the instructions with durations of other rows, and closes as written. The experiments with it were less well foreseen: the loop's removal left 0.7 us over 10.44, of which moving the first copy between the gates gave back 0.44.
- **Mix, +12: wrong, +102, outside its bounds of −5 and +45.** The failing step is the sentence that the gated tile "comes by one more engine but TensorE's order asks for it later". It looked at TensorE's order only. The same loop had been looked for in project and found; in mix nobody walked from VectorE's unfold to ScalarE's copy, through the gate and its table load, the shift, the normalising and back, though the lists stood in the code. And the lock that had been costed in kernel rows was not costed here, where GpSimd got four new operations that read SBUF: beside them a shift of 0.16 us takes 0.75. One move of `invert` brought back 62 us of the stage, and in the kernel with all repairs, whose only other edit in mix is that of `scale_gate`, 42 more.
- **Rivals.** Rival (c) ended slower than before by a frequency over 24.1. The columns came to 23.91, on the winning side of that point, and the kernel still lost, because the point rested on +200 for the other stages and they took +312. With those the columns would have had to stay under 27.55 + 8/56 − 312/56 = 22.1. Rival (d), every loop at its upper bound, was the nearest, 5329; its sum took the bounds, and two of them were no bounds.
- **The chance of 0.08 for slower** came from (c) alone. What was missing was a rival in which TensorE stops being full in all four stages; the trace of before had it full in each, and the folds put one more engine between two of its products.

## What to carry to other kernels

When work is taken off the engine that bounds a loop, walk the loop through the other engines in the order of their lists, in every stage the edit touches and not only in the one where the loss is expected; a loop is closed when each wait in it stands behind the one before. When a load is moved, price its landing from the busiest moment of its neighbours, and if TensorE waits 2 or 3 us for it, count some microseconds of products behind the wait at the lower clock. Where two costs lie beside each other, an experiment that takes away one shows only what the other doesn't hold: take away both before a suspect is acquitted.

## What the runs showed of the hardware

- After TensorE's wait of 3.96 us that ended at 2101.02 the granted clock was 0.54 for 3.7 us, and after the one of 2.88 that ended at 2124.94 the taps' products took 1.99 again. With what follows it, the wait of 2.85 us a frequency cost 4.57, 1.6 times its own length. A shorter wait had the same sequel: behind the 1.97 us that ended at 316.68 in the kernel with fills the granted clock was 0.50 for 3.4 us.
- Products on opposite halves of the array run as pairs for fp32 in both directions, and an image with two changes of shape takes 2.05 us, at a clock of 1.00 and with no gap from 1500 to 2300.
- A table load of ScalarE (1.28 us) waited for the input of the activation behind it: the one at 3492.20 begins after 1.51 us of waiting for VectorE's mx_u_pre, so it is on the path in full, though it has no tile as its input.
- VectorE's operation with two SBUF inputs kept its length (682 ns) beside GpSimd fills that write only, and was held by GpSimd's sums (up to 2705 ns); VectorE's cast, with one input, was lengthened by both (340 ns beside fills, 542 beside sums; 219 where GpSimd only casts).
- The same sum of 112x1024 columns takes GpSimd 2.4 to 2.6 us and VectorE 1.22.
